# Message passing over a graph: one gathered tile of 32 is fetched row by row from the SP and ScalarE queues

## What is computed

```python
msg_in = jnp.concatenate([nodes[row], nodes[col], edge_features], axis=-1)
messages = _mlp(msg_in, mW1, mb1, mW2, mb2)          # relu(x @ W1 + b1) @ W2 + b2, hidden 128
aggregated = jax.ops.segment_sum(messages, col, num_segments=nodes.shape[0])
upd_in = jnp.concatenate([nodes, aggregated], axis=-1)
return _mlp(upd_in, uW1, ub1, uW2, ub2)
# and at the end: x = _layernorm(x + that)
```

## Time and profile before

| | us |
|---|---|
| median of 3 runs | 2049.36 (2049.04 to 2050.01) |
| the profiled execution | 2048.59 |
| its span, first to last instruction | 2046.8 |

### The profile page before, as it was taken

How to read it: one execution, slowest core, us unless ns; L and a number is a source line. 1 busy time by engine, 2 the same in 40 slices (tenths; PEclk the granted TensorE clock), 3 DMA queues, 4 the chain that set the end, 5 groups by cost and what they waited for, 6 DMA issues and landing times.

```text
span 2046.8 us, 34700 instructions
## 1 busy us (share of the span) xinstructions
PE 1438.8 (70%) x10080; PEld 1316.0 (64%) x10080; DVE 871.9 (43%) x2220; ACT 562.8 (27%) x929; POOL 1480.1 (72%) x1572
## 2 busy tenths in 40 slices
PE   7986666776666766766677767677677767667675
PEld 7976666666656666665666656566566656566664
DVE  3353333333333343333333444445444444444444
ACT  2332222222222222222222333233333333333332
POOL 0567777777777777777777777777777777777774
PEclk9997777777787687778876878787888778877877
DMA  8732323322232233223222223233223322232321
GB/s 212 206 100 79 80 78 77 82 78 78 80 80 78 78 80 80 77 78 81 79 76 72 80 78 82 75 81 79 76 78 80 80 75 81 78 80 75 82 78 46
DMA packets 167585, 173.49 MB, mean 85 GB/s; under 512 B 65654, under 2 KB 129433, under 8 KB 167209
## 3 DMA queue, kind: packets, MB, share of 16 engines
q0 software_dynamic: 50016, 102.53, 19.4%
q1 hardware_dynamic: 104088, 63.37, 11.2%
q10 hardware_dynamic: 13458, 7.31, 1.6%
HBM read 156.74 MB, written 16.31 MB: 85 GB/s over the span
## 4 chain that ended last, share of the span: by engine, by line
POOL 68%; issue 24%; PE 5%; POOLq 1%; DMA 1%; DVE 0%; ACT 0%; SPq 0%; ACTq 0%; DVEq 0%
POOL ag L223 68%; PE bank L367 4%; DMA xc<-x_t 1%; PE bank L260 0%; POOLq L209 0%; PE bank L270 0%; POOLq L220 0%; POOLq L773 0%; PE bank L634 0%; DMA ag<-src_table,slot_idx 0%; DMA dst_table<-picks 0%; DMA picks<-edge_t 0%; PE bank L247 0%; PE bank L640 0%; PE bank L274 0%
## 5 line engine op out<-in xcount | busy, mean ns | idle before, releaser
L223 POOL DMA_INDIRECT ag<-src_table,slot_idx x1563 | 1479.1, 946 | 543.8 <-issue 485.3
L270 PE MATMUL bank<-oh,hid 128*128 128x96 f32 x3128 | 533.5, 326 | 414.2 <-DVE xc L329 370.5
L270 PEld LDWEIGHTS bank<-oh,hid 128*128 128x128 f32 x3128 | 479.9, 234 | 472.7 <-ACT hid L291 425.0
L312 DVE TENSOR_TENSOR hid<-bank,ag 128x512 f32<-128x512 f32 x391 | 270.3, 691 | 886.6 <-DMA ag<-src_table,slot_idx 751.0
L260 PE MATMUL bank<-picked,picks 128*128 128x128 f32 x3128 | 582.5, 345 | 3.7 <-DMA picks<-edge_t 3.1
L291 ACT ACTIVATE hid<-hid 128x512 f32<-128x512 f32 x391 | 245.7, 628 | 1164.8 <-DVE hid L312 1164.8
L260 PEld LDWEIGHTS bank<-picked,picks 128*128 128x128 f32 x3128 | 520.7, 252 | 6.9 <-issue 3.3
L285 ACT ACTIVATE picks<-bank 96x512 f32<-96x512 f32 x391 | 226.2, 579 | 181.8 <-PE bank L247 132.3
L299 DVE TENSOR_TENSOR oh<-iota,rel 128x384 f32<-128x384 f32 x391 | 218.0, 558 | 117.9 <-PE bank L274 61.1
L247 PE MATMUL bank<-ident_bf,oh 128*96 128x128 bf16 x1564 | 193.6, 260 | 53.2 <-DVE oh L299 52.6
L247 PEld LDWEIGHTS bank<-ident_bf,oh 128*96 128x96 bf16 x1564 | 147.4, 155 | 103.4 <-DVE oh L299 65.7
(11 more groups left out here) (55 smaller groups left out, 349.4 us busy)
## 6 DMA issues: line engine op xcount, KB each, us to landing
picks<-edge_t SPq DMA_DIRECT2D x391, 64.0 KB
ag<-src_table,slot_idx POOLq DMA_INDIRECT x1563
picked<-dst_table SPq DMA_DIRECT2D x391, 48.0 KB
src_table<-ag SPq DMA_DIRECT2D x25, 256.0 KB, 3.5
dst_table<-picks SPq DMA_DIRECT2D x17, 256.0 KB, 2.6
xc<-x_t ACTq DMA_DIRECT2D x4, 800.0 KB, 16.0
resid<-x_rows SPq DMA_DIRECT2D x24, 128.0 KB
out<-resid ACTq DMA_DIRECT2D x24, 128.0 KB
```

The source lines that it names most:

```text
L223: pool.indirect_dma_start(out=ag[:, k, j * DH:(j + 1) * DH], out_offset=None, in_=src_table, in_offset=bass.IndirectOffsetOnAxis(ap=slot_i ...
L270: nc.tensor.matmul(ps_a[q][:, 0:WIN], hid[:, q, j * DH:(j + 1) * DH], oh[:, r, j * WIN:(j + 1) * WIN], start=(j == 0), stop=(j == TPG - 1))
L312: dve.tensor_tensor(hid[:, q, :], ps_h[q][:, :], ag[:, k, :], ALU.add).then_inc(s_pre, 1)
```

## The change

The last of the four tiles of the group at k = 5 is no longer gathered in laps 1 to 48. Its 128 rows of 512 bytes are copied by 128 DMAs of one row each, 64 issued by SP and 64 by ACT, straight to `ag[row, 5, 384:512]`. The address of each is computed from a register. POOL issues 31 gathers a lap in place of 32 (48 fewer in all).

The row numbers come as a new input (`src_own`). DVE converts them to int16, SP stores them to device memory and reads them back as one long row in one partition (`own_row`). From there a register load (TENSOR_LOAD) brings them to registers, 8 at a time on ACT and 9 or 10 at a time on SP.

On SP they stand behind the window and edge loads of k = 1 to 7, 9 or 10 rows each, the first of a lap behind a new wait for `add_source` of the previous lap's group 5. On ACT 8 rows stand behind every `relu`, from k = 5 of one lap to k = 4 of the next. DVE waits for all of them on eight semaphores ahead of `add_source` at k = 5. SP and ACT also wait, once, for the source table and for `own_row` before their loops.

```diff
+OWN_K = 5
+OWN_SP = P // 2
+OWN_ACT = P - OWN_SP
+OWN_SEMS = 4
+OWN_J = TPG - 1
+OWN_AT = OWN_J * DH
...
+        def own_indices(eng, lap, at, n):
+
+            return nc.values_load_multi_w_load_instructions(
+                own_row[0:1, ds(lap * P + at, n)], engines=(eng,), min_val=0, max_val=N_NODES - 1,
+                skip_runtime_bounds_check_because="an index of a node")[1]
...
+        def own_cut(step, steps, rows):
+
+            return step * rows // steps, (step + 1) * rows // steps
+
+        def own_row_dma(eng, row, node):
+
+            return eng.dma_start(ag[row:row + 1, OWN_K, OWN_AT:], src_table[ds(node, 1), :])
+
+        def own_rows_sp(sp, k, lap):
+
+            if k == 0 or not fills_own(lap):
+                return
+            if k == 1:
+                sp.wait_ge(s_pre, (lap - 1) * UNROLL + OWN_K + 1)
+            a, b = own_cut(k - 1, UNROLL - 1, OWN_SP)
+            for n, node in enumerate(own_indices(ET.SP, lap, a, b - a)):
+                own_row_dma(sp, a + n, node).then_inc(s_own_sp[(k - 1) // 2], 16)
+
+        def own_rows_act(k, lap):
+
+            act = nc.scalar
+            lap += k >= OWN_K
+            if fills_own(lap):
+                step = (k - OWN_K) % UNROLL
+                a, b = own_cut(step, UNROLL, OWN_ACT)
+                for n, node in enumerate(own_indices(ET.Activation, lap, OWN_SP + a, b - a)):
+                    own_row_dma(act, OWN_SP + a + n, node).then_inc(s_own_act[step // 2], 16)
+
+        def wait_own_rows(eng, lap):
+
+            for n in range(OWN_SEMS):
...
+                eng.wait_ge(s_own_sp[n], lap * sp_rows * 16)
+                eng.wait_ge(s_own_act[n], lap * act_rows * 16)
...
-            wait(dve, s_gathered[k], (lap + 1) * 16 * TPG - 16 * missing)
+            wait(dve, s_gathered[k], gathered_of(k, lap) - 16 * missing)
+            if has_own(k, lap):
+                wait_own_rows(dve, lap)
...
-                        gather(pool, i * UNROLL + k, k)
+                        gather(pool, i * UNROLL + k, k, TPG - (k == OWN_K))
...
+            sp.dma_start(own_i, src_own).then_inc(s_own, 16)
...
-            sp.wait_ge(s_scratch, 64)
+            sp.wait_ge(s_own_h, 1)
+            sp.dma_start(own_dram, own_h).then_inc(s_scratch, 16)
+            sp.wait_ge(s_scratch, 80)
+            sp.dma_start(own_row[:, :], own_dram.rearrange("(o t) e -> o (t e)", o=1)).then_inc(s_own_row, 16)
...
                             load_window(sp, g, k, bases[k])
                             load_edges(sp, g, k)
+                        own_rows_sp(sp, k, i)
...
                             relu(g, k)
+                        own_rows_act(k, i)
```

More of the change, by code:

```diff
@@ L44, with build @@
 assert (ITERS - 1) * UNROLL < G_END <= GROUPS and 2 * GPP == UNROLL
-def build(nc, x_rows, x_t, src_first, src_all, dst_groups, dst_tiles, edge_t,
+def build(nc, x_rows, x_t, src_first, src_all, src_own, dst_groups, dst_tiles, edge_t,
           mw1, mb1, mw2, mb2, uw1, ub1, uw2, ub2, out):
@@ L51, in build @@
     bf16 = mybir.dt.bfloat16
+    i16 = mybir.dt.int16
     ALU = mybir.AluOpType
@@ L75, in build @@
         lag_dram = dram("window_lag", (GROUPS,))
+        own_dram = dram("own_rows", (ITERS, P), i16)
         agg_dram = dram("agg_rows", (AGG_ROWS, AGG_W))
@@ L123, in build @@
         oh = sb("oh", [P, RING, TPG * WIN])
+        own_row = sb("own_row", [1, ITERS * P], i16)
         hid = sb("hid", [P, 2, TPG * DH])
@@ L128, in build @@
         dst_g_real = resid[0:GROWS, GPP * GE:2 * GPP * GE]
+        own_i = resid[0:ITERS, 3 * GPP * GE:3 * GPP * GE + P].bitcast(i32)
+        own_h = resid[0:ITERS, 3 * GPP * GE + P:3 * GPP * GE + P + P // 2].bitcast(i16)
         base_all = resid[:, 2 * GPP * GE:2 * GPP * GE + GROUPS]
@@ L164, in build @@
         s_flag = sem("s_flag")
+        s_own = sem("s_own")
+        s_own_h = sem("s_own_h")
+        s_own_row = sem("s_own_row")
         s_rel = sem("s_rel")
@@ L178, in build @@
         s_window = [sem(f"s_window{i}") for i in range(RING)]
+        s_own_sp = [sem(f"s_own_sp{n}") for n in range(OWN_SEMS)]
+        s_own_act = [sem(f"s_own_act{n}") for n in range(OWN_SEMS)]
         s_oh = sem("s_oh")
@@ L213, in upper_halves, with has_own, fills_own, gathered_of @@
             return ap.bitcast(bf16).rearrange("p (n two) -> p n two", two=2)[:, :, 1]
+        def own_indices(eng, lap, at, n):
+            return nc.values_load_multi_w_load_instructions(
+                own_row[0:1, ds(lap * P + at, n)], engines=(eng,), min_val=0, max_val=N_NODES - 1,
+                skip_runtime_bounds_check_because="an index of a node")[1]
+        def has_own(k, lap):
+            return k == OWN_K and not (isinstance(lap, int) and lap == 0)
+        def fills_own(lap):
+            return not isinstance(lap, int) or 0 < lap < ITERS
+        def own_cut(step, steps, rows):
[20 more added lines that the diff above has]
+            for n in range(OWN_SEMS):
+                sp_rows = sum(b - a for k in range(1, UNROLL) if (k - 1) // 2 == n
+                              for a, b in [own_cut(k - 1, UNROLL - 1, OWN_SP)])
+                act_rows = sum(b - a for step in range(UNROLL) if step // 2 == n
+                               for a, b in [own_cut(step, UNROLL, OWN_ACT)])
+                eng.wait_ge(s_own_sp[n], lap * sp_rows * 16)
+                eng.wait_ge(s_own_act[n], lap * act_rows * 16)
+        def gathered_of(k, lap):
+            return 16 * TPG + lap * 16 * (TPG - (k == OWN_K))
         def gather(pool, g, k, tiles=TPG):
@@ L552, in general_vector @@
             dst_table_stored(dve)
+            dve.wait_ge(s_own_row, 16)
             dve.wait_ge(s_src, 16)
@@ L774, in windowed @@
                     for k in range(UNROLL):
-                        gather(pool, i * UNROLL + k, k)
+                        gather(pool, i * UNROLL + k, k, TPG - (k == OWN_K))
                 for g in range((ITERS - 1) * UNROLL, G_END):
-                    gather(pool, g, g % UNROLL, min(TPG, T_END - g * TPG))
+                    gather(pool, g, g % UNROLL, min(TPG - (g % UNROLL == OWN_K), T_END - g * TPG))
             windows_fit(pool, windowed, general_pool)
@@ L828, in windowed @@
                 dst_table_stored(sp)
+                src_table_stored(sp)
+                sp.wait_ge(s_own_row, 16)
                 def lap(i):
@@ L871, in windowed @@
                 dst_table_stored(act)
+                src_table_stored(act)
+                act.wait_ge(s_own_row, 16)
                 copy_oh(0, 0)
@@ L916, in _ @@
                                      ).then_inc(s_base, 1)
+            dve.wait_ge(s_own, 16)
+            dve.tensor_copy(own_h, own_i).then_inc(s_own_h, 1)
             dve.wait_ge(s_base, 1)
@@ L1063 @@
         "src_all": src_tiles,
+        "src_own": np.ascontiguousarray(src_p.reshape(ITERS, UNROLL, TPG, P)[:, OWN_K, OWN_J, :]),
         "dst_groups": dst_p.reshape(GROWS, GPP * GE),
```

## The result

| | median us | ratio to the kernel before | 95% interval |
|---|---|---|---|
| before | 2049.69 | | |
| changed | 2647.86 (2647.32 to 2649.07, 4 runs) | 1.292 | 1.2897 to 1.2942 |

A forecast was written before the change was run, and what follows sets the result against it. POOL was taken to bound the kernel before, SP's and ACT's queues after. Laps 1 to 25 add 25 x 8.0 = 200 us, laps 26 to 48 add 23 x 12.3 = 283: 2048.6 + 483 = 2532, rounded 2530; range 2200 to 2800.

The forecast's parts named there:

- The bound and its change: POOL's gathers bind; 48 fewer by 1.25 save 60 us, making 1989 us if POOL's 38.75 us lap stayed the bound.
- SP's lap: SP's queue: windows, edges, base load, register loads and 64 rows sum to 47.5 us, 48.0 with a chunk of x.
- The row's price: One row's DMA on either queue: 0.17 + 0.20 = 0.37 us from start to start, between 0.34 and 0.52.
- two savings: In a row's DMA: 0.18 us less for one row, 0.11 less for a register address; both together would give 0.14.
- ACT's lap: ACT's queue: 47.5 us in plain laps, 52.3 with an update, including a 2.2 us stall once a lap.
- the cover: On ACT, the 1.8 us register load covers only relu's 0.63; the update's 4.8 us lose their idle-time cover.
- The sum: Whole kernel: laps 1 to 25 lose 200 us by SP, laps 26 to 48 lose 283 by ACT; 2532, rounded 2530.
- (1): ACT's aligned register loads are fast, its laps 37.5 and 42.3 us, SP's 47.5 sets all: 2421 us; chance 0.20.
- (2): Contiguity alone makes reads fast on both queues, 0.53 us; the kernel takes 2027 or 2070 us; chance 0.12.
- (3): Only engines differ: SP reads fast, ACT like DVE; ACT sets both kinds of lap, 2519 us; chance 0.10.
- (4): Row DMAs cost their upper price or pile up on one DMA engine: 2800 to 3000 us; chance 0.08.
- the signs that I had named: ACTq and SPq solid, rows 0.37 us apart, loads 1.8 and 2.0, POOL waiting for slot_idx, laps 48 then 52.

The follow-up runs named there:

- e7: Changed kernel without register loads, each row DMA copying a fixed row whose address is written in the program: 2007.63 us, 0.979 of the kernel before.
- e3b: Changed kernel with ACT's 64 rows a lap and their register loads left out, SP's rows alone: 2644.21 us, 1.289 of the kernel before.
- e4b: Changed kernel with SP's rows left out, ACT's rows alone: 2431.56 us, 1.185 of the kernel before.
- e2: Changed kernel with row numbers as four-byte words, SP reading from 0, 9, 18 and so on: 3662.83 us beside 2675.90 before, not used.
- e1b: Changed kernel with row numbers as four-byte words, every read beginning on a multiple of 8: 2213.92 us, 1.080 of the kernel before.

## Why the prediction was right, point by point

**The bound and its change.** Right: POOL bound before, and its 60 us of saved gathers were worth nothing, because SP's lap passed POOL's 38.75. e7, where only the queues' work was cut, gives 43 of the 60 back. (The 3.9 us that ACT waits are of one group; the page of the kernel before has 1164.8 us in 391 waits, 3.0 each. Nothing hung on it.)

**SP's lap.** The steps held and one term, the rows, was too small. In a plain lap of 52.4 us, with each instruction counted to the start of the next one, it comes to (us):

| | forecast | measured |
|---|---|---|
| windows and edges | 8.2 | 8.4 |
| base load and turn | 0.9 | 1.3 |
| load of x | 0.5 | 0.6 |
| seven register loads | 14.7 | 15.1 |
| 64 rows | 23.7 | 27.0 |
| sum | 48.0 | 52.4 |

Register loads: 2.0 us forecast for nine values, 2.018 measured. Rows: 0.37 forecast, 0.412 measured, 64 x 0.042 = 2.7 us a lap, and 0.6 more for the first rows behind a load and the step from the last row. The base load takes 0.697 us in the changed kernel, 0.525 before; why, no run shows. With no x to load the lap is 51.8 against 47.5 forecast.

```profile
L407 SPq TENSOR_LOAD <-base_row x49: 540/697/708, 102.8 to 2571.4; - x49
```

**The row's price.** This is where my reasoning was wrong in itself. I had added two savings, one row for many (0.18) and a register address for a fixed one (0.11), and placed the price at 0.17, near their sum. They don't add: register-addressed 0.228, fixed 0.247 before and 0.252 in e7. A one-row DMA costs about the same either way. The row nearest in shape, 0.247, was nearer to the truth, and with it the prediction's own sum gives 2776, too much again, nearly all of it through the next point.

**ACT's lap.** Wrong by mechanism in the laps with an update. I had ACT set them at 52.3 us; it alone would need 49.0, and SP's 51.8 sets them (e3b, e4b). The step that failed is the cover: a register load of 1.9 us hides `copy_oh` as well as `relu`, and more than half of the update's 4.8 us, of which some 2 are left. Two errors of opposite sign met, SP's row too cheap and ACT's lap too long. It is luck that the second half came out at 12 us a lap above before, as forecast. In the first half no such luck helped: 12.6 us a lap where 8.0 were forecast.

**The sum.** Forecast 200 + 283 = 483 us. Measured by laps: 25 x 12.6 + 23 x 11.7 = 315 + 269 = 584 of the span's 600. The remaining 16 us are a term that I didn't have, the start. Before, SP's base loads of laps 1, 2 and 3 begin at 120.1, 138.1 and 167.8 us, so SP's laps 1 and 2 take 18.0 and 29.7 us in place of 40; POOL had begun to gather at 59.4 us and was ahead. In the changed kernel they begin at 119.4, 173.4 and 225.9 us: 54.0 and 52.4. These two laps lose 34 us more than the sum by laps counts. About 7 come back in the lap in which the updates open (47.3 us before, 51.9 after) and 8 in the last, since from SP's last base load to the end it is 72.0 us before and 75.8 after. What is left lies within the rounding of the laps.

**The rivals.** (1), fast aligned reads on ACT, fell with 1.887 us for two-byte values. (2), contiguity alone makes reads fast, fell with the change itself, and for words with e2: nine contiguous words from a shifted start took 2.04. (3), the engine decides, fell with e1b. (4), the DMA engines, fell with e7. Most of the signs that I had named came true: POOL waits for `slot_idx` (642 us), reads of 1.9 and 2.0 us, SP's queue solid, laps of 52 us from lap 26 on. Three didn't: the row's step was 0.41 in place of 0.37, the laps before lap 26 took 52.4 us in place of 48, and ACT's queue isn't solid, with eight groups of 5.53 us in a lap of 52.4 (706.06 - 700.53 in its timeline).

**A price for each register.** Nine two-byte values at 2.018 us and nine shifted words at 2.035 come to 0.22 a value, eight aligned words at 0.69 to 0.09. The Trainium skill, "Runtime: NRT & Kernel Launch", section "Instruction fetch mechanics", gives some 200 ns a register even in bulk. It speaks of loads from HBM, and those here read SBUF. The first two agree with it, the aligned words don't. By that rule e1b would have taken about as long as the change; it took 434 us less.

## What to carry to other kernels

Work moved to a "free" queue must be priced in that queue's time: instructions by their start-to-start step, register loads included, against the length of a lap, since the busy share of an engine doesn't show it. Read register values as whole words from an aligned start, eight at a time, and give a queue only as much as it can average below the engine that binds; here half the work won 1.1% where all of it lost 29%. Two savings seen in two comparisons should not be added without a row that has both.

## What the runs showed of the hardware

- A register load of eight words that begins on a multiple of 8 takes 0.53 to 0.72 us on SP and ACT, one of nine words from 36 on SP 0.91; eight or nine two-byte values, or words from the other starts, take 1.85 to 2.05, some 0.23 a value.
- ACT's activations and table loads run beside a register load on its queue: one of 1.91 us covers two activations of 1.2 us together, one of 1.88 us a table load of 1.28.
- A DMA of one row of 512 bytes is two packets in its queue, 6144 for ACT's 3072.
- A one-row DMA of 512 bytes takes SP 0.228 us to issue with a register address and 0.252 with a fixed one; with the register operations one starts 0.41 us after the other.
- An indirect gather of 64 rows takes 0.90 us where 128 take 0.94.
- With row DMAs in every lap the mean gather is 12 ns longer (958 against 946), through single gathers of up to 1.3 us.
